# Graph network kernel: layer norm moved into the adjacency loop, degrees summed without self loops, softplus moved behind the first inputs

## The reference

```python
x = x + gnn(layernorm(x), edges, W, b)      # layernorm over features
# gnn:
loops = arange(n); src = concat(edges[0], loops); dst = concat(edges[1], loops)
deg = segment_sum(1, dst)                   # a second self loop is in here
dis = rsqrt(maximum(deg, 1))
for l in range(3):
    h = x @ W[l]
    x = relu(segment_sum(h[src] * (dis[src] * dis[dst]), dst) + b[l])
```

## Time and profile before

| | us |
|---|---|
| median of 3 runs | 988.98 |
| lowest and highest | 986.0, 990.35 |
| the profiled execution's own time | 987.39 |
| its span, first to last instruction | 985.6 |
| TensorE busy | 853.1 (87%) |
| VectorE busy | 509.0 (52%) |
| ScalarE busy | 234.1 (24%) |
| mean granted TensorE clock | 0.943 of 2.4 GHz |

### The profile page before, as it was taken

How to read it: one execution, slowest core, us unless ns; L and a number is a source line. 1 busy time by engine, 2 the same in 40 slices (tenths; PEclk the granted TensorE clock), 3 DMA queues, 4 the chain that set the end, 5 groups by cost and what they waited for, 6 DMA issues and landing times.

```text
span 985.6 us, 12333 instructions
## 1 busy us (share of the span) xinstructions
PE 853.1 (87%) x3638; PEld 572.8 (58%) x3639; DVE 509.0 (52%) x934; ACT 234.1 (24%) x483; POOL 78.6 (8%) x127
## 2 busy tenths in 40 slices
PE   4887699999999949679998688999998989999890
PEld 2444478888888826368887543544554545555440
DVE  7988681431431797890246958434343343433362
ACT  2555321431431024242112121102121211212110
POOL 2000000000000300000000010111011110110180
PEclk9999779999999978889999598999999999999996
DMA  4720000000000010001001120427754593314163
GB/s 141 223 101 1 1 1 1 0 1 1 1 1 1 27 45 1 1 1 43 1 3 60 66 91 0 168 99 276 279 176 154 190 352 92 148 53 154 39 178 118
DMA packets 38647, 80.98 MB, mean 82 GB/s; under 512 B 7304, under 2 KB 7554, under 8 KB 38602
## 3 DMA queue, kind: packets, MB, share of 16 engines
q1 hardware_dynamic: 27850, 60.55, 17.9%
q0 software_dynamic: 6720, 12.49, 4.3%
q10 hardware_dynamic: 4032, 7.34, 2.0%
HBM read 101.97 MB, written 16.92 MB: 121 GB/s over the span
## 4 chain that ended last, share of the span: by engine, by line
PE 70%; DVE 11%; DMA 5%; ACT 5%; issue 4%; POOL 2%; ACTq 1%; SPq 0%; DVEq 0%; POOLq 0%
PE PS L893 18%; PE PS L1108 13%; PE PS L923 8%; PE PS L1141 7%; PE PS L827 5%; PE PS L1016 5%; DMA WB<-in_b 3%; PE PS L962 3%; PE PS L1096 3%; PE PS L1126 2%; ACT CTR L607 1%; ACT YF L754 1%; POOL GA L576 1%; POOL GB L576 1%; DMA GB<-y_dram,slot_i 1%
## 5 line engine op out<-in xcount | busy, mean ns | idle before, releaser
L893 PE MATMUL PS<-CTR,YH 125*128 125x500 f32 (+1 forms) x480 | 167.0, 363 | 3.8 <-DVE YL L1405 3.4
L893 PE MATMUL PS<-CTR,YL 125*128 125x500 f32 (+1 forms) x480 | 165.1, 359 | 0.0
L1108 PE MATMUL PS<-WB,YF 128*128 x448 | 150.4, 489 | 7.5 <-DMA WB<-in_b 5.0
L1108 PEld LDWEIGHTS PS<-WB,YF 128*128 128x128 f32 x448 | 84.0, 190 | 76.7 <-issue 24.7
L893 PEld LDWEIGHTS PS<-CTR,YH 125*128 125x128 f32 x480 | 92.1, 192 | 22.5 <-DVE YL L1405 9.8
L893 PEld LDWEIGHTS PS<-CTR,YL 125*128 125x128 f32 x480 | 92.6, 193 | 12.6
L1141 PE MATMUL PS<-WB,YF 128*128 x168 | 79.4, 609 | 12.5 <-ACT YF L754 11.2
L827 PE MATMUL PS<-ET 125*128 125x130 f16 x494 | 71.0, 291 | 15.7 <-ACT CTR L607 8.2
L1438 DVE TENSOR_TENSOR ZL<-PS,ZH 128x500 fp32r<-128x500 f32 (+1 forms) x36 | 21.1, 591 | 93.1 <-ACT ZH L657 93.1
L754 ACT COPY YF<-PS 128x384 f32<-128x384 f32 (+1 forms) x38 | 18.1, 477 | 213.8 <-PE PS L1118 213.8
L827 PEld LDWEIGHTS PS<-ET 125*128 125x128 f16 x494 | 40.4, 116 | 47.0 <-ACT CTR L607 26.5
(11 more groups left out here) (324 smaller groups left out, 1214.8 us busy)
## 6 DMA issues: line engine op xcount, KB each, us to landing
WB<-in_w SPq DMA_DIRECT2D x28, 1536.0 KB
WB<-in_w SPq DMA_DIRECT2D x28, 768.0 KB
WB<-in_b SPq DMA_DIRECT2D x28, 384.0 KB
y_dram<-YF ACTq DMA_DIRECT2D x28, 256.0 KB
y_dram<-XTF SPq DMA_DIRECT2D x1, 4352.0 KB, 14.5
X<-in_x SPq DMA_DIRECT2D x1, 2500.0 KB
xn_dram<-XN SPq DMA_DIRECT2D x1, 2500.0 KB
out<-X SPq DMA_DIRECT2D x10, 250.0 KB
```

The costliest lines, as they stand in the source:

```text
L893: mm = nc.tensor.matmul(dest, lhs, rhs, start=(t == 0 and h == 0), stop=(t == NT - 1 and h == 1))
L1108: mm = nc.tensor.matmul(PS[:, 2 * k + h, 0:INTER], xgt[:, k, f, :], WB[:, bass.ds(off + (f * H2 + h * INTER), INTER)], start=(f == 0), sto ...
```

## The change

Five edits. (1) The table with three one-hot sets for each group becomes one with two and a separate one with one (oh_next), so VectorE does three operations a batch. (2) In the loop, at batches 2 to 11 VectorE does one bn_stats of x each; at batch 12 the bn_aggr and epsilon, at batch 16 the reciprocal and the shift (-mean / deviation). ScalarE does the square root at group 60, and one Identity with scale and shift for each tile at batches 18 to 27, into a new tile XHAT. (3) TensorE waits for all copies itself and sums the degrees of CTR without the second self loop; that is added on VectorE after the degrees are copied. The square root gets a bias of 1 and the clamp of counts loses its -1. (4) The first layer's YH is XHAT times dis on ScalarE, YL one operation on VectorE. (5) The softplus follows the first layer's inputs on both engines. The declarations of the new tiles and semaphores are left out of the diff.

```diff
@@ -36,6 +36,9 @@
...
 LOADS = 8
+STATS_AT = 2
+DEV_AT = STATS_AT + 10
+SHIFT_AT = DEV_AT + 4
@@ -173,15 +177,19 @@
...
         srcf, dstf, hi, lo, where = [carve(NCH) for _ in range(5)]
-        later = carve(2 * NG).rearrange("p (a g) -> p a g", a=2)
+        later = src_i.bitcast(F32).rearrange("p (a g) -> p a g", a=2)
...
-        key16 = carve(NG * (OWN + 1), F16).rearrange("p (g x) -> p g x", x=OWN + 1)
+        key16 = carve(NG * OWN, F16).rearrange("p (g x) -> p g x", x=OWN)
+        next16 = carve(NG * 2, F16).rearrange("p (g x) -> p g x", x=2)
         iota_lo = carve(128 * OWN, F16).rearrange("p (n x) -> p n x", x=OWN)
-        iota_key = carve(KEYS * (OWN + 1), F16).rearrange("p (n x) -> p n x", x=OWN + 1)
+        iota_key = carve(KEYS * OWN, F16).rearrange("p (n x) -> p n x", x=OWN)
+        iota_next = carve(KEYS, F16).rearrange("p (n x) -> p n x", x=2)
         lo_bufs = [carve(BATCH * 128 * OWN, F16) for _ in range(RING)]
-        key_bufs = [carve(BATCH * KEYS * (OWN + 1), F16) for _ in range(RING)]
+        key_bufs = [carve(BATCH * KEYS * OWN, F16) for _ in range(RING)]
+        next_bufs = [carve(BATCH * KEYS, F16) for _ in range(RING)]
         oh_lo = [m.rearrange("p (g n x) -> p g n x", g=BATCH, x=OWN) for m in lo_bufs]
-        oh_key = [m.rearrange("p (g n x) -> p g n x", g=BATCH, x=OWN + 1) for m in key_bufs]
+        oh_key = [m.rearrange("p (g n x) -> p g n x", g=BATCH, x=OWN) for m in key_bufs]
+        oh_next = [m.rearrange("p (g n) -> p g n", g=BATCH) for m in next_bufs]
@@ -475,9 +484,9 @@
...
                       allow_small_or_imprecise_dtypes=True).then_inc(const_done, 1)
-            pool.iota(iota_key[:, :, 0:OWN], pattern=[[1, KEYS], [0, OWN]], base=0, channel_multiplier=0,
+            pool.iota(iota_key[:, :, :], pattern=[[1, KEYS], [0, OWN]], base=0, channel_multiplier=0,
                       allow_small_or_imprecise_dtypes=True).then_inc(const_done, 1)
-            pool.iota(iota_key[:, :, OWN:OWN + 1], pattern=[[1, KEYS], [0, 1]], base=1, channel_multiplier=0,
+            pool.iota(iota_next[:, :, :], pattern=[[2, KEYS // 2], [1, 2]], base=1, channel_multiplier=0,
@@ -607,28 +616,35 @@
...
                                ).then_inc(placed, 1)
+                if g == BATCH * DEV_AT:
+                    sqrt_of_var(0)
+                t = (g - BATCH * (SHIFT_AT + 2)) // BATCH
+                if g % BATCH == 0 and 0 <= t < NT:
+                    act.wait_ge(shift_ready, 1)
+                    nc.scalar.activation(XHAT[0:NP, t, :], X[0:NP, t, :], ACT.Identity, scale=rstd[0:NP, t:t + 1],
+                                         bias=shift[0:NP, t:t + 1]).then_inc(val_ready, 1)
+            act.wait_ge(degcol_ready, 1)
+            nc.scalar.activation(dis[0:NP, :], PS[0:NP, 3, 0:NT], ACT.Sqrt, bias=ones[0:NP, 0:1]).then_inc(sd_ready, 1)
+            def split_weight(k, raw, name, count):
+                act.wait_ge(load[name], count)
+                nc.scalar.copy(WH[:, :, :], raw).then_inc(wh_ready, 1)
+            act.wait_ge(load["w12"], 32)
+            act.wait_ge(dis_ready, 1)
+            for t in range(NT):
+                act.wait_ge(val_ready, t + 1)
+                nc.scalar.activation(YH[0:NP, t, :], XHAT[0:NP, t, :], ACT.Copy, scale=dis[0:NP, t:t + 1]
+                                     ).then_inc(yh_ready, 1)
+            act.wait_ge(zeroed, 16)
+            act.wait_ge(deg_ready, len(SPLITS))
+            split_weight(0, WRAW[:, :, :], "w0", 16)
...
             nc.scalar.activation(clampv[:, 4, :, :], clampv[:, 3, :, :], ACT.Ln).then_inc(sp_ln, 1)
-            sqrt_of_var(0)
-            act.wait_ge(degcol_ready, 1)
-            nc.scalar.activation(dis[0:NP, :], PS[0:NP, 3, 0:NT], ACT.Sqrt).then_inc(sd_ready, 1)
-            def split_weight(k, raw, name, count):
-                act.wait_ge(load[name], count)
-                nc.scalar.copy(WH[:, :, :], raw).then_inc(wh_ready, 1)
-            act.wait_ge(zeroed, 16)
-            act.wait_ge(deg_ready, len(SPLITS))
-            split_weight(0, WRAW[:, :, :], "w0", 16)
-            act.wait_ge(load["w12"], 32)
-            for t in range(NT):
-                act.wait_ge(val_ready, t + 1)
-                nc.scalar.copy(YH[0:NP, t, :], val[0:NP, t % 2, :]).then_inc(yh_ready, 1)
@@ -825,7 +841,8 @@
...
                 return nc.tensor.matmul(PS[0:128, g % 6, 0:KEYS], oh_lo[lb % RING][0:CHUNK, c // OWN % BATCH, :, c % OWN],
-                                        oh_key[b % RING][0:CHUNK, g % BATCH, :, x], start=start, stop=stop)
+                                        oh_key[b % RING][0:CHUNK, g % BATCH, :, x] if x < OWN
+                                        else oh_next[b % RING][0:CHUNK, g % BATCH, :], start=start, stop=stop)
@@ -860,6 +877,7 @@
...
+            pe.wait_ge(placed, NG)
@@ -878,6 +896,7 @@
...
             mm.then_inc(degcol_ready, 1)
+            pe.wait_ge(loops_ready, 1)
@@ -1228,7 +1247,7 @@
...
                 v.tensor_scalar(mv[0:NP, :, 1], mv[0:NP, :, 1], EPS, None, ALU.add).then_inc(var_ready, 1)
-                dve.wait_ge(sd_ready, k + 1 if k == 0 else k + 2)
+                dve.wait_ge(sd_ready, k + 2)
@@ -1261,20 +1280,20 @@
...
             v.memset(wbase_i[0:1, NG:], 0)
-            v.memset(key16[0:CHUNK, NG - 1:NG, OWN:OWN + 1], 0.0)
+            v.memset(next16[0:CHUNK, NG - 1:NG, :], 0.0)
...
             chunks = lambda m: m[0:CHUNK, :].rearrange("p (g x) -> p g x", x=OWN)
-            v.tensor_tensor(key16[0:CHUNK, :, 0:OWN], chunks(where),
+            v.tensor_tensor(key16[0:CHUNK, :, :], chunks(where),
...
                                         in1=wbase[0:CHUNK, 0:NG - 1], op0=ALU.add, op1=ALU.subtract))
-            link(v.tensor_tensor(key16[0:CHUNK, 0:NG - 1, OWN], later[0:CHUNK, 0, 0:NG - 1], later[0:CHUNK, 1, 0:NG - 1],
-                                 ALU.mult))
+            twice = lambda k: later[0:CHUNK, k, 0:NG - 1].rearrange("p (g o) -> p g o", o=1).to_broadcast([CHUNK, NG - 1, 2])
+            link(v.tensor_tensor(next16[0:CHUNK, 0:NG - 1, :], twice(0), twice(1), ALU.mult))
@@ -1284,16 +1303,38 @@
...
                                 ALU.is_equal)
-                dims = [CHUNK, BATCH, KEYS, OWN + 1]
-                return v.tensor_tensor(oh_key[b % RING][0:CHUNK],
-                                       iota_key[0:CHUNK].rearrange("p n (o x) -> p o n x", o=1).to_broadcast(dims),
-                                       key16[0:CHUNK, groups, :].rearrange("p g (o x) -> p g o x", o=1).to_broadcast(dims),
+                dims = [CHUNK, BATCH, KEYS, OWN]
+                v.tensor_tensor(oh_key[b % RING][0:CHUNK],
+                                iota_key[0:CHUNK].rearrange("p n (o x) -> p o n x", o=1).to_broadcast(dims),
+                                key16[0:CHUNK, groups, :].rearrange("p g (o x) -> p g o x", o=1).to_broadcast(dims),
+                                ALU.is_equal)
+                dims = [CHUNK, BATCH, KEYS // 2, 2]
+                return v.tensor_tensor(oh_next[b % RING][0:CHUNK].rearrange("p g (n x) -> p g n x", x=2),
+                                       iota_next[0:CHUNK].rearrange("p n (o x) -> p o n x", o=1).to_broadcast(dims),
+                                       next16[0:CHUNK, groups, :].rearrange("p g (o x) -> p g o x", o=1).to_broadcast(dims),
...
                 onehots(b).then_inc(onehot_ready, 1)
+                t = b - STATS_AT
+                if t == 0:
+                    dve.wait_ge(load["x"], 16)
+                if 0 <= t < NT:
+                    ins = v.bn_stats(stats[0:NP, t, 0, :], X[0:NP, t, :])
+                    if t == NT - 1:
+                        link(ins)
+                if b == STATS_AT + NT:
+                    for t in range(NT):
+                        ins = v.bn_aggr(mv[0:NP, t, :], stats[0:NP, t, 0, :])
+                    link(ins)
+                    v.tensor_scalar(mv[0:NP, :, 1], mv[0:NP, :, 1], EPS, None, ALU.add).then_inc(var_ready, 1)
+                if b == SHIFT_AT:
+                    dve.wait_ge(sd_ready, 1)
+                    link(v.reciprocal(rstd[0:NP, :], sd[0:NP, :]))
+                    v.scalar_tensor_tensor(out=shift[0:NP, :], in0=mv[0:NP, :, 0], scalar=-1.0, in1=rstd[0:NP, :],
+                                           op0=ALU.mult, op1=ALU.mult).then_inc(shift_ready, 1)
@@ -1359,6 +1400,7 @@
...
+            v.memset(bad[:, 3:4], 0.0).then_inc(counts_ready, 1)
@@ -1369,61 +1411,43 @@
...
-            self_loops(ALU.add, counts_ready)
+            for s, (c0, w) in enumerate(SPLITS):
+                dve.wait_ge(deg_ready, s + 1)
+                ins = v.tensor_copy(invc[:, c0:c0 + w], PS[:, s, 0:w])
+            ins.then_inc(deg_copied, 1)
+            self_loops(ALU.add, loops_ready)
+            dve.wait_ge(sd_ready, 2)
+            v.reciprocal(dis[0:NP, :], dis[0:NP, :]).then_inc(dis_ready, 1)
+            dve.wait_ge(dis_ready, 1)
+            def low_part(m, t, source):
+                dve.wait_ge(yh_ready, m + 1)
```

(54 more changed lines are left out.)

## The result

Over 20 runs each, the changed kernel has a median of 991.54 us (987.26 to 999.87) and the kernel before 988.33 (983.42 to 990.49). The ratio is 1.0036, with a 95% interval of 1.0021 to 1.0052: 2 to 5 us slower. The forecast was 995.0 in a range of 988.5 to 1000, most likely slower by over 0.5%; the result is slower, but by 3.2 us, where the sum said 6.9.

What follows compares the result with a forecast made beforehand. ScalarE's copies were taken to set the loop, with TensorE nearly idle for about 33 us behind it. Loop +19.1 and -12.2 behind it gave +6.9 on 987.4, 994.3 us, put at 995.0; range 988.5 to 1000.

Steps and rivals of the forecast that it cites:

- the lower bound of 26: Load of x: complete at 26 us if undisturbed on five full engines; as a rival, sum +1.4, chance 0.16.
- The stall: In the loop at batch 2: VectorE waits for x, making ScalarE's fifteenth copy late by 11.5 us.
- The rest of the loop: From the fifteenth copy to the last: statistics, TensorE restart, square root and Identities add 7.6 us.
- The restart of TensorE: In the loop after the wait for x: TensorE resumes at half clock, +1.0 us (0 to 3).
- The root: ScalarE's square root in the loop: a table load of 1.28 us and 0.2, together +1.5.
- The ten Identities: ScalarE's scaled tiles in the loop: 0.45 us each, +4.5 in all.
- From the last copy to the linear matmul: Behind the loop: aggregation starts 6.3 us earlier, and faster tiles bring the gain to 12.2 us.
- The rival of TensorE keeping its clock: Behind the loop: degree matmuls take 6 us, 2 to 3 less, total 992; chance 0.12 shared with x at 29 to 30.
- Behind it: After the aggregation's start: the moved softplus, later root table load and degrees without self loops cost nothing.
- The most likely case: Whole kernel: slower by over 0.5% (4.9 us), chance 0.64.
- the case of no change to be told: Whole kernel: within 0.5% (4.9 us) of the kernel before, chance 0.28.
- The faster rival: Load of x: in place when batch 2 asks, so no stall or cold restart; 982 us, chance 0.08.

Runs made afterwards that it cites:

- e12: Changed kernel with one more SyncE wait, so nothing is issued behind the load of x until x is complete: 986.8 us, 0.9982 of the kernel before.
- e1: Changed kernel with the load of x cut in two, 120 partitions and 5: 983.3 us, 0.9938 of the kernel before.
- e2: Kernel before with the load of x cut in two, 120 partitions and 5: 988.5 us, ratio 0.9993.
- e5: Changed kernel with self loops again added before the degrees are summed: 994.7 us, 1.0062 of the kernel before.
- e7: Kernel before with only the self loops moved behind the degree copies: 986.6 us, ratio 0.9968.
- e6: Changed kernel with the softplus put back ahead of the degree copies: 992.9 us, 1.0034 of the kernel before.
- e3: Changed kernel with the statistics at batches 9 to 18 instead of 2 to 11, root and Identities later too: 980.3 us, 0.9898 of the kernel before.

## Why the prediction was right, and where it was not

**When VectorE asks for x, and when x is there: right.** Three batches end at 17.27 (17.3 forecast); x is there at 32.2 (31.4). e12 confirms the lower bound of 26 and so both halves of the argument, five full engines and the slowing from 18 us by what moves beside x. The rule of the Trainium skill that was set against that bound (DMA: Bandwidth & Descriptors, "Why a DMA increments its semaphore by 16 and not by 1") gives five engines for 125 rows, and the third of a busy share in e12 agrees to the end of the load. What it does not give is the rate of fifteen engines: e1's 206 GB/s decides there. Nor does being on five engines and ahead in their rings speak against 26 by itself, as the prediction had it: x was both in e12 and landed at 26. What makes it late is in the rows: 128 GB/s at a share of 0.33 are about 24 GB/s for each busy engine, and 220 GB/s with all sixteen busy are 14 (estimates from the earlier trace rows).

**The stall: 12.8 for 11.5.** Of the difference 0.8 are the landing (32.2 for 31.4).

**The rest of the loop: 4.1 for 7.6. This is the step that failed in size.** Copy by copy the lateness against the kernel before is 12.8 us at the fifteenth, 13.2 at the 35th, 15.5 at the 55th, 14.3 at the 61st, 15.6 at the 65th, 13.5 at the ninetieth and 16.9 at the 140th. From that:

- VectorE's pace costs 0.4 up to the 35th copy, for 0.6.
- The restart of TensorE costs nothing, for 1.0. The granted clock was at 0.50 from the stall to behind the loop, and still TensorE did its three weight loads a group in 0.24 us, as it did at a granted 1.00 before (two stretches of the changed kernel, in the loop and in the columns, then a group's loads):

```profile
60.00:80.00 20.00, 17.20 (x120) 9.60 (x121) 17.87 (x30) 12.95 (x44) 0.00 (x0) 0.50 0.00 1
123.00:125.00 2.00, 1.49 (x14) 1.29 (x12) 1.51 (x8) 0.00 (x0) 0.00 (x0) 1.00 0.00 0
```

```profile
84.86 0.24 PEld L843 LDWEIGHTS PS<-ET 125*128 125x128 f16 x3 [0.18 <-ACT CTR L616]
```

  The loads wait for ScalarE's copy: its 0.43 a copy is longer than what TensorE needs. In e12 the record shows 1.00 in the wait (its stretch above) and in the loop, and from the twentieth copy to the last the lateness grew there by 4.2 us, as much as in the changed kernel under 0.50. The loop of e2 is that of the kernel before: from 30 to 90 us the record shows 0.50 in e2 and 1.00 in the kernel before, TensorE is busy for 53.0 and 52.4 us, and the last copies start at 96.42 and 96.43.
- The root costs 1.27, for 1.5: its wait is covered and the table load is not. The load starts 0.02 behind a copy and the root 0.01 behind the load. The Trainium skill (ScalarE: Activation LUTs, "What ACT_TABLE_LOAD costs") adds a drain of 1.38 us to a switch; this trace has the 1.28 and no room for the drain, and the measurement decides.
- Slow loads of window places: three of them (1.64 to 1.93 us copy to copy) ahead of the 61st, 69th and 77th copy before, two ahead of the 37th and 45th after, at 47.5 and 52.5 us. They come with the transfers, 44 to 57 us, and not with a certain copy, and a kernel that is late meets fewer of them. This gives back about 1. The prediction had the slow loads in the rate of the loop, as if they came with the copies, and so put this term at nothing.
- The ten Identities cost 3.4, for 4.5. ScalarE's timeline at one of them:

```profile
86.13 0.26 ACT L616 CAST CTR<-PS 125x120 f32 x1 [0.16 <-PE PS L843]
86.29 0.82 ACT L624 ACTIVATE XHAT<-X,shift,rstd 125x512 f32<-125x512 f32 x1
87.01 0.25 ACT L616 CAST CTR<-PS 125x120 f32 x1
```

  0.88 from copy to copy where 0.43 is usual: 0.45 each, as forecast. But in three of the ten a load of window places (0.30) went on beside the Identity, and these 0.9 us are saved.

**From the last copy to the linear matmul: -13.4 for -12.2.** Right to within 0.6 us in each step but the columns. Degree matmuls begin 2.0 behind the last copy's end (1.4 forecast) and take 7.97 (8.6). The columns take 2.35 where 3.75 was put: their granted clock was 1.00 (the second stretch above), where it fell to 0.50 in the columns before. TensorE stood still for 0.51 us ahead of them, where it was 3.31 before. The rival of TensorE keeping its clock had the degree matmuls in 6 us, which did not come; only the columns came out its way. The clock fell right behind them, to 0.50, and rose near 133, as in the kernel before. The first aggregation matmul is 15.1 behind the last copy's end, for 16.3: 7.5 us of the gain (6.3 forecast). The other 5.9, as forecast, come between the first aggregation matmul and the linear one.

The prediction read half clock into the degree matmuls of the kernel before from their 8.59 us. The granted clock there says 1.00, and the two don't go together (the kernel before, then two stretches of the changed kernel):

```profile
102.00:104.00 2.00, 2.00 (x6) 1.58 (x6) 1.61 (x5) 1.52 (x3) 0.00 (x0) 1.00 0.00 0
117.00:119.00 2.00, 2.00 (x6) 1.64 (x5) 0.00 (x0) 0.00 (x0) 0.00 (x0) 0.50 0.00 0
120.00:122.00 2.00, 2.00 (x11) 1.66 (x10) 0.68 (x1) 0.00 (x0) 0.00 (x0) 1.00 0.04 8
```

In 2 us there are six of these equal matmuls at 0.50 and eleven at 1.00 in the changed kernel, but six under a recorded 1.00 in the kernel before. So a recorded 1.00 doesn't prove full speed in these traces, nor does it in the loop, and the durations are the firmer evidence.

Of the -13.4 edit 3 is worth 1.5 to 1.9 (e5, e7) and edit 5 nothing (e6). How the rest divides between edits 2 and 4 was not tried.

**Behind it: nothing, as forecast.** The linear matmul is 48.2 behind the aggregation's start, with no bank waited for, and the second layer's is 3.45 late, as the first.

**Sum.** 12.8 + 4.1 - 13.4 = +3.5 for +6.9. The sign and the mechanism were right: the gain behind the loop is real, and the loop loses more. The most likely case, slower by over 0.5% (0.64), did not come; 0.36% lies in the case of no change to be told, which had 0.28. The loop was put 3.5 too high and the gain behind it 1.2 too low, and the stall, 1.3 too low, made up for part of that. The faster rival (x in place when asked for) is what e3 shows when the asking is moved: 9.5 us faster.

## What to carry to other kernels

Before work is moved forward into idle slots of an engine, look up when its data lands, not when it was first used: a load that nobody waited for may be the last thing to come. Here seven batches of delay turned 3 us lost into 9.5 us won. And put the added work on the engine that does not set the loop's pace; the same ten tiles cost 3.2 us on ScalarE and nearly nothing on VectorE.
